# Context laid out with its features first, score maxima taken from two banks, one context load asked for earlier

## The reference

```python
x = x + xattn(layernorm(x), ctx, ctx)   # 32 query heads over 8 key/value groups of width 16, 512 context rows per batch
x = x + attn(layernorm(x))              # the same heads over the 32 tokens of the batch, causal, with rotary embedding
x = x + ffn(layernorm(x))               # one 512x512 matrix of 3-bit weights with a norm per 32, and a bias
```

## Time and profile before

| what | us |
|---|---|
| median of 3 runs | 349.91 |
| lowest and highest run | 349.44 and 350.54 |
| span of the profiled execution | 348.0 |
| PE busy in that span | 332.6 |
| DVE, ACT, POOL busy | 223.0, 192.1, 112.3 |

### The profile page before, as it was taken

The page is one execution under the profiler, slowest core; times in us unless marked ns, Lnnn a source line. Parts: engine busy times, 40 slices in busy tenths (PEclk is TensorE's granted clock), DMA queues, the critical chain, the costliest instruction groups (busy, mean ns, idle before and its releaser), DMA issues.

```text
span 348.0 us, 8374 instructions
## 1 busy us (share of the span) xinstructions
PE 332.6 (96%) x2930; PEld 240.3 (69%) x2930; DVE 223.0 (64%) x392; ACT 192.1 (55%) x369; POOL 112.3 (32%) x202
## 2 busy tenths in 40 slices
PE   7999785999999999999999999999899999999996
PEld 3764553777777777777777777777656866876664
DVE  1877673767667667586676766765766349876552
ACT  3553232676676666775766677765965612434220
POOL 1340831341331322413313123133551144663320
PEclk9999998999999999999999999999999999999999
DMA  7990298865777649869697599795940000000002
GB/s 268 406 126 0 63 208 191 173 116 153 108 186 153 121 154 125 176 155 113 172 179 99 156 112 215 156 182 160 130 55 2 2 6 6 6 9 6 2 32 90
DMA packets 40796, 41.52 MB, mean 119 GB/s; under 512 B 20112, under 2 KB 35472, under 8 KB 38672
## 3 DMA queue, kind: packets, MB, share of 16 engines
q1 hardware_dynamic: 40336, 41.00, 56.4%
q10 hardware_dynamic: 432, 0.13, 0.2%
HBM read 24.07 MB, written 1.05 MB: 72 GB/s over the span
## 4 chain that ended last, share of the span: by engine, by line
PE 85%; DVE 5%; DMA 2%; SPq 2%; ACT 2%; issue 1%; POOL 1%; ACTq 0%; DVEq 0%; POOLq 0%
PE b_d L1032 8%; PE b_c L1091 8%; PE b_s L1053 8%; PE b_v L1007 4%; PE b_c L1227 4%; PE b_k L1009 4%; PE b_k L1007 4%; PE b_k L1008 4%; PE b_v L1009 4%; PE b_v L1008 4%; PE b_x L979 4%; PE b_t L979 3%; DMA kstack<-kparts 2%; PE b_c L1212 2%; PE b_v L1058 2%; PE b_v L1117 1%
## 5 line engine op out<-in xcount | busy, mean ns | idle before, releaser
L789 DVE TENSOR_REDUCE negmax<-b_s 128x1 f32<-128x512 f32 x128 | 88.0, 688 | 70.6 <-PE b_s L1053 63.1
L594 ACT ACTIVATE region<-b_c 128x512 f32<-128x512 f32 x128 | 74.6, 597 | 53.6 <-PE b_c L1091 32.3
L1053 PE MATMUL b_s<-kstack,qstack 96*128 96x512 bf16 x128 | 49.5, 387 | 7.9 <-DMA kstack<-kparts 3.6
L1091 PEld LDWEIGHTS b_c<-qstack,kstack 108*128 108x128 bf16 x512 | 32.7, 98 | 26.6 <-issue 21.7
L1091 PE MATMUL b_c<-qstack,kstack 108*128 108x128 bf16 x512 | 50.5, 222 | 0.0
L476 POOL TENSOR_TENSOR mwide<-negmax,zeros 128x4 bf16<-128x4 f32 x32 | 6.4, 199 | 108.7 <-DVE negmax L789 108.7
L467 POOL TENSOR_TENSOR kparts<-kres,zeros 128x512 bf16<-128x512 f32 x16 | 18.9, 1180 | 40.3 <-DVE kres L774 40.3
L1007 PE MATMUL b_v<-cT_h,wkv_h 128*128 128x512 f32 x64 | 31.3, 489 | 0.0
L1032 PE MATMUL b_d<-region,vaug 128*17 128x128 f32 x1024 | 31.1, 273 | 0.0
L1007 PE MATMUL b_k<-cT_h,wkv_h 128*128 128x512 f32 x64 | 30.8, 481 | 0.0
L1032 PEld LDWEIGHTS b_d<-region,vaug 128*17 128x17 f32 x1024 | 26.6, 97 | 1.8 <-issue 0.2
(11 more groups left out here) (380 smaller groups left out, 663.8 us busy)
## 6 DMA issues: line engine op xcount, KB each, us to landing
cx<-in_ctx_dram SPq DMA_DIRECT2D x16, 1024.0 KB, 4.9
kstack<-kparts SPq DMA_DIRECT2D x96, 128.0 KB, 4.5
qstack<-region SPq DMA_DIRECT2D x76, 32.0 KB, 3.0
xs<-in_x_dram SPq DMA_DIRECT2D x1, 1024.0 KB, 8.1
region<-in_L_xattn_Wq_dram SPq DMA_DIRECT2D x1, 1024.0 KB, 10.2
cx<-in_L_xattn_Wo_dram SPq DMA_DIRECT2D x8, 128.0 KB, 4.3
cx<-in_L_attn_Wq_dram SPq DMA_DIRECT2D x1, 1024.0 KB, 5.4
region<-in_L_attn_Wo_dram SPq DMA_DIRECT2D x8, 128.0 KB, 7.4
```

The source lines that it names most:

```text
L594: nc.scalar.activation(pT[:, g], b_c[g % 2][:].rearrange("p (a n) -> p a n", a=KT), ACT.Exp, scale=SCALE).then_inc(exp_ready, 1)
L789: nc.vector.tensor_reduce(negmax[:, n % 2, g:g + 1], b_s[:], AX, ALU.max, negate=True).then_inc(max_ready, 1)
L1053: nc.tensor.matmul(b_s[:], qstack[0:STACK, g, n % 4], kstack[0:STACK, n % 4, g], start=True, stop=True).then_inc(s_ready, 1)
L1091: last = nc.tensor.matmul(b_c[g % 2][:, P * a:P * a + P], kstack[0:ROWS, m % 4, g, P * a:P * a + P], qstack[0:ROWS, g, m % 4], start=True, ...
```

## The change

The host hands over the context with features first (each batch transposed), Wq and Wk already in the order that the kernel used to make on the chip, and both output matrices in the order of the heads, so that their loads are one DMA each in place of eight. On the chip:

- `load_ctx` brings 4 features x 512 rows to each partition; ACT and DVE make `cT_h` and `cT_l` straight from that tile in SBUF. All 256 context transposes on PE go (16 in the opening for batch 0, 240 of line 979). Loads now wait for `ctx_low` (the chunks have been split) instead of `ctx_transposed`.
- Scores of odd groups go to bank `b_x` in slots before 14 (`score_bank`), so PE waits for the maximum two groups back, not one.
- Batch 0's context comes as four DMAs with a semaphore each. Batch 3's context is loaded in the opening, before the first query DMAs, not in slot 0.
- The reordering copies of Wq and the strided ones of Wk go. PE's warm-up is 9 matmuls, not 14, and the four after the context turn go.

```diff
+        first_ctx = [sem(f"first_ctx{c}") for c in range(C - 1)]
...
+        def score_bank(n, g, trip):
+
+            return b_x if g % 2 and (looped(trip) or n < B - 2) else b_s
...
-                sp.dma_start(cx[:, m % 2], ctx_d[4 * trip + m].rearrange("(p a) d -> p a d", a=KT)).then_inc(ctx_loaded[m % 2], 16)
+                sp.dma_start(cx[:, m % 2], ctx_d[4 * trip + m].rearrange("(p c) k -> p c k", c=C)).then_inc(ctx_loaded[m % 2], 16)
...
-                load_ctx(0, 0)
-                sp.dma_start(wkv_raw[:, 1], xwv_d.rearrange("(c p) m -> p c m", p=P)).then_inc(wv_loaded, 16)
+                first = ctx_d[0].rearrange("(p c) k -> p c k", c=C)
+                for c in range(C):
+                    sp.dma_start(cx[:, 0, c], first[:, c]).then_inc((*first_ctx, ctx_loaded[0])[c], 16)
+                sp.dma_start(wkv_raw[:, 1], xwv_d.rearrange("(p c) m -> p c m", c=C)).then_inc(wv_loaded, 16)
...
-                sp.wait_ge(ctx_transposed, C)
+                sp.wait_ge(ctx_low, C)
                 load_ctx(2, 0)
...
+                sp.wait_ge(ctx_low, 2 * C)
+                load_ctx(3, 0)
                 for part, done in ((0, q_high), (2, q_low)):
                     sp.wait_ge(done, R)
...
-                if live(n + 3, trip):
-                    sp.wait_ge(ctx_transposed, transposed)
+                if live(n + 3, trip) and (looped(trip) or n > 0):
+                    sp.wait_ge(ctx_low, halved)
                     load_ctx(n + 3, trip)
...
-                    sp.wait_ge(ctx_transposed, C * (B - 1))
-                    for g in range(G):
-                        sp.dma_start(wo[HD * g:HD * g + HD],
-                                     xwo_d[R * HD * g:R * HD * (g + 1)].rearrange("(r d) n -> d r n", r=R)).then_inc(weights_loaded, 16)
+                    sp.wait_ge(ctx_low, C * (B - 1))
+                    sp.dma_start(wo, xwo_d).then_inc(weights_loaded, 16)
...
-                pool.wait_ge(xwq_loaded, 16)
-                for c in (2, 3):
-                    nc.gpsimd.tensor_copy(wq_dg[:, c].rearrange("p r (d g) -> p r d g", g=G),
-                                          xwq[:, c].rearrange("p (g r d) -> p r d g", g=G, r=R)).then_inc(wq_ordered, 1)
...
-                        wait(act, ctx_transposed, C, m, c + 1, trip)
+                        if c == 0:
+                            wait_ring(act, ctx_loaded, m, trip)
                         wait(act, v_chunk, C, m - 1, c + 1, trip)
-                        nc.scalar.activation(cT_h[:, c], b_tx[c % 2][:], ACT.Copy).then_inc(ctx_high, 1)
+                        nc.scalar.activation(cT_h[:, c], cx[:, m % 2, c], ACT.Copy).then_inc(ctx_high, 1)
...
-                        nc.vector.tensor_reduce(negmax[:, n % 2, g:g + 1], b_s[:], AX, ALU.max, negate=True).then_inc(max_ready, 1)
+                        nc.vector.tensor_reduce(negmax[:, n % 2, g:g + 1], score_bank(n, g, trip)[:], AX, ALU.max, negate=True).then_inc(max_ready, 1)
...
-                        nc.vector.tensor_tensor(cT_l[:, c], b_tx[c % 2][:], cT_h[:, c].bitcast(F32), ALU.subtract).then_inc(ctx_low, 1)
+                        nc.vector.tensor_tensor(cT_l[:, c], cx[:, m % 2, c], cT_h[:, c].bitcast(F32), ALU.subtract).then_inc(ctx_low, 1)
...
-                        wait(pe, max_ready, G, n, g, trip)
-                        nc.tensor.matmul(b_s[:], qstack[0:STACK, g, n % 4], kstack[0:STACK, n % 4, g],
+                        wait(pe, max_ready, G, n, g - 1 if looped(trip) or n < B - 2 else g, trip)
+                        nc.tensor.matmul(score_bank(n, g, trip)[:], qstack[0:STACK, g, n % 4], kstack[0:STACK, n % 4, g],
                                          start=True, stop=True).then_inc(s_ready, 1)
...
-                    for second in range(2):
-                        ctx_ahead(n, g, second, trip)
-                        if n == B - 2:
+                    if n == B - 2:
+                        for second in range(2):
                             weight_part(g // 2, 2 * (g % 2) + second)
...
-                warm(14)
-                pe.wait_ge(ident_loaded, 16)
-                first_context(0)
-                first_context(1)
-                first_context(2)
-                first_context(3)
-                warm(4)
+                warm(9)
                 pe.wait_ge(wk_split, 1)
...
-                next_context(1, 0)
-                next_context(1, 1)
-                first_queries_of(0)
-                next_context(1, 2)
-                first_queries_of(1)
-                next_context(1, 3)
-                first_queries_of(2)
-                first_queries_of(3)
+                for r in range(R):
+                    first_queries_of(r)
...
-                next_context(2, 0)
```

More of the change, by code:

```diff
@@ L391, in slot @@
                 if looped(trip):
-                    passed, transposed, split = (
+                    passed, halved, split = (
                         sp.snap(step * trip + base) for step, base in
@@ L396, in slot @@
                 else:
-                    passed, transposed, split = G * (n - 1), C * m + C, m + 1
-                if live(n + 3, trip):
-                    sp.wait_ge(ctx_transposed, transposed)
+                    passed, halved, split = G * (n - 1), C * m + C, m + 1
+                if live(n + 3, trip) and (looped(trip) or n > 0):
+                    sp.wait_ge(ctx_low, halved)
                     load_ctx(n + 3, trip)
@@ L709, in opening @@
                 act.wait_ge(wk_loaded, 16)
[L710 to L711 removed]
+                nc.scalar.activation(wkv_h[:, 0], wkv_raw[:, 0], ACT.Copy).then_inc(wk_high, 1)
                 context(0, 0)
@@ L970, in _ @@
         def _(pe):
-            def ctx_part(m, c, a, trip):
-                if a == 0:
-                    if c == 0:
-                        wait_ring(pe, ctx_loaded, m, trip)
-                    wait(pe, ctx_low, C, m, c - 1, trip)
-                    if not looped(trip) and (m, c) == (1, 1):
-                        pe.wait_ge(xhT_ready, 1)
-                piece = nc.tensor.transpose(b_tx[c % 2][:, P * a:P * a + P], cx[:, m % 2, a, P * c:P * c + P], ident[:])
-                if a == KT - 1:
-                    piece.then_inc(ctx_transposed, 1)
             def weight_part(c, t):
@@ L1212, in warm @@
                     nc.tensor.matmul(b_c[1][:], zeros[:, 0:P], zeros[:], start=True, stop=True)
-            def first_context(c):
-                if c == 0:
-                    pe.wait_ge(ctx_loaded[0], 16)
-                for a in range(KT):
-                    last = nc.tensor.transpose(b_first[c][:, P * a:P * a + P], cx[:, 0, a, P * c:P * c + P], ident[:])
-                last.then_inc(ctx_transposed, 1)
             def first_queries_of(r):
                 pe.wait_ge(xhT_ready, TILES)
-                pe.wait_ge(wq_ordered, C)
+                pe.wait_ge(xwq_loaded, 16)
                 count(pe, q_res, r - 1)
                 for c in range(C):
-                    last = nc.tensor.matmul(b_c[r % 2][:], wq_dg[:, c, r], xhT[:, c], start=(c == 0), stop=(c == C - 1))
+                    last = nc.tensor.matmul(b_c[r % 2][:], xwq[:, c, r], xhT[:, c], start=(c == 0), stop=(c == C - 1))
                 last.then_inc(q_summed, 1)
-            def next_context(m, c):
-                for a in range(KT):
-                    ctx_part(m, c, a, 0)
             def opening():
                 pe.wait_ge(zeros_ready, 1)
-                warm(14)
-                pe.wait_ge(ident_loaded, 16)
-                first_context(0)
-                first_context(1)
-                first_context(2)
-                first_context(3)
-                warm(4)
+                warm(9)
                 pe.wait_ge(wk_split, 1)
@@ L1290 @@
     arrays = {name: _np.ascontiguousarray(inputs[name]) for name in _INS}
+    turned = lambda name, shape, axes: _np.ascontiguousarray(arrays[name].reshape(shape).transpose(axes))
+    arrays["ctx_4096"] = turned("ctx_4096", (B, KEYS, D), (0, 2, 1))
+    arrays["L0_xattn_Wq"] = turned("L0_xattn_Wq", (D, G, R, HD), (0, 2, 3, 1)).reshape(D, R, P)
+    arrays["L0_xattn_Wk"] = turned("L0_xattn_Wk", (D, G, HD), (0, 2, 1)).reshape(D, KV)
+    for name in ("L0_xattn_Wo", "L0_attn_Wo"):
+        arrays[name] = turned(name, (G, R, HD, D), (0, 2, 1, 3)).reshape(KV, R, D)
     arrays["L0_ffn_weight_q3"] = arrays["L0_ffn_weight_q3"].view(_np.int32)
```

52 lines of the change are left out of this document (16 added, 36 removed).

## The result

The changed kernel takes 337.89 us (median; 335.09 to 338.57), the kernel before on the same chip 349.68 (348.64 to 350.54): a ratio of 0.9654, interval 0.9612 to 0.9697. It is faster, as forecast, but by 12 us and not by 28, and 337.9 lies above the range of 317 to 333. The profiled span went from 348.0 to 336.7 us (the execution of 338.57).

What follows compares the result with a forecast made beforehand. PE was taken to bound the middle slots. Opening 3.0, slot 0 3.3, slot 1 3.4, middle slots 17.5 and slot 13 0.6 sum to 27.8 us off the 348.0 span: 320.2, so 322 us as median, range 317 to 333.

Steps and rivals of the forecast that it cites:

- rival 1: Middle slots: DVE's split stands behind POOL's key parts at the shared port, PE waits 1.2 us a slot; 336 us, chance 0.12.
- rival 2: Middle slots: ACT and DVE chains take over, PE waits for values and exponentials, slot stays 13.2 us; 330 us, chance 0.10.
- Rival 3: Every slot's first score waits for late-landing keys, so the kernel gets slower; 360 us with landings of 10, chance 0.03.
- I charge 0.2: Middle slots: lost cover at the turn of the values costs 0.2 us, making the slot 12.5 us instead of 12.33.
- I place the last split's end near 10.8: 1 us earlier: Opening: batch 0's context splits end 1 us earlier; part of the 3.0 us forecast gain to the first score.
- ACT then waits for Wv: Opening: between context splits ACT waits for Wv, whose DMA now stands behind the four context quarters.
- The stated lower bound of 0: Opening: the 3.0 us gain falls to 0 if PE's clock is still at the lower level in the first projections.
- The stop: Slot 0: DVE's split, reading SBUF twice, stands until POOL's multiply is done, 39.4 to 43.05 us.
- Nothing but DVE bounds it: Slot 0: DVE's 8 maxima, 4 splits and a copy alone set its length; forecast gain 3.3 us.
- a landing of 4.5 makes 10.2, under 12.5: Middle slots: keys made 5.7 us after the slot's first score land within the slot, so nothing is charged.
- took back 1.4 us for the clock: Slot 1: the 1.4 us cost of PE's half-clock start disappears; part of the 3.4 us forecast gain.
- batch 3's early load: Slot 0: loading batch 3's context before the queries costs a 0.6 us issue and lets slot 1's keys land at 48.8.

Runs made afterwards that it cites:

- the opening's two edits: Changed kernel with Wv's DMA right behind Wk's and seven more warm-up matmuls before the third projection chunk of batch 0; together, first score at 41.95 us (44.02 without).
- POOL's weights: Changed kernel with POOL's multiply and subtraction over the feed-forward weights moved out of the opening, in eight parts each in slots 0 and 1; 333.0 us.
- POOL's parts: Changed kernel with POOL's two multiplies and subtractions of 2048 elements cut into eight of 256 each, at the same places; 334.5 us.
- one bank: Changed kernel with one score bank instead of two by turns, each score waiting for the maximum just before it; 343.3 us.

## Why the prediction was wrong

The mechanism was right: PE bounded the slots, the turns were worth 0.22 us a pair, and a middle slot could go to 12.46. Neither of the rivals that stand for the middle (rival 1 at 336, rival 2 at 330) was the cause as they put it, and that 337.9 lies nearest to rival 1 is chance: in the middle slots no split that delayed PE is seen, and ACT is at 9.31 of 12.84 us. Rival 1 did name a late value copy, but by the port, and rival 2 DVE's chain, but by ACT's lines. Rival 3, dismissed at 0.03, was half right: keys land late, but in slots 2 and 14 only.

- **Middle slots, 3.8 of the missing 16.5 us.** The step "I charge 0.2" looked at PE's wait for ACT's copy before the turn alone. Behind the turn DVE's copy frees `b_v`, and ahead of it in DVE's order stand a maximum and the normalisation; the prediction doesn't name that wait. It costs 0.38 us a slot, shown by the run with the copy first. The 0.2 itself was about right: 12.46 in that run, against 12.33 without any wait.
- **Opening, 5.4 us.** "I place the last split's end near 10.8: 1 us earlier", with the statistics of x right behind, never asked when x lands. It had landed at 10.3 in the kernel before, and the change sends it 1.3 us later. "ACT then waits for Wv" was said and priced at next to nothing; it was 3.26 us. And the half clock, put down as a bound only, was real: the removed turns and warm-up matmuls were what PE did before these projections. The stated lower bound of 0 excluded a loss without a reason.
- **Slot 0, 2.0 us.** The stop came as forecast; but from its end (49.02) to slot 1's first score it is 8.2 us, where the prediction's eleven DVE instructions make 6.7: PE, at half clock until 55, bounds the rest. "Nothing but DVE bounds it" left that out, though the earlier trace rows has the same thing in slot 1.
- **Slot 1, 5.0 us.** The one sum for the keys, "a landing of 4.5 makes 10.2, under 12.5", stands with the middle slots and takes the median of all key DMAs; for slot 1, in which 1.2 MB is sent ahead of them, the wait for keys was put at nothing. With 8.31 the sum is 14.0, and slot 1 lasted 14.11. I also took back 1.4 us for the clock; PE stood still again, one slot later. And batch 3's early load, costed as a help, loses 2.3 us to slot 2's product against the changed kernel's profile (0.8 to 3.2 against the six runs that leave this stretch alone).
- **Slot 13, 0.4 us.** Keys again, 0.24 us of wait at slot 14's first score, which the sum had at nothing (and 4 x 0.22 less 0.2 is 0.7, not 0.6); what makes that wait small here and up to 2.6 us in other runs stays open. From slot 14 nothing was lost, as forecast.

With the opening's two edits, the copy, the keys, POOL's weights and the last layer's Wk and Wv put in the new order, the change gives 327.0 us. What keeps it from 322 is the opening (42.2 us to the first score; 38.6 was forecast), and slot 2, whose context is late once the keys go first (14.24 us).

## What to carry to other kernels

When work leaves the engine that bounds a loop, list for every buffer who frees it and what stands ahead of the freeing instruction in its own engine's order; the next wait is there, and a swap of two instructions can be worth as much as part of the change. Take a transfer's landing from the stretch in question, with the bytes that go out beside it, never as a median over the kernel; a shorter slot has the same bytes in less time. In an opening, ask of every input when it lands before asking when an engine could start on it.

## What was not expected of the hardware

- In the opening the granted clock is printed as 1.00 (12 to 14 us, and 14 to 16) while the same matmuls stand 0.42 us apart. The trace holds no record of the clock there before 17.76 us, and where it has none the column prints 1.00. From the first record on the two agree: in slot 2 (73.37 to 74.23) the column shows 0.50, with 0.43 between starts. So ahead of the first record the distance between starts, not the column, tells the clock.
- The clock's course in the opening differs between runs that are alike up to there. After the change and in three others the matmuls stand 0.42 us apart until 17.3 to 17.9. In four (POOL's parts, one bank, batch 3's context in slot 0, POOL's weights moved) they stand 0.23 apart from 7.6 us at the latest; the next ones, behind the third split, start 3.9 to 4.7 us later, and the clock is at 0.50 from 11.5 to 13.3 on until 15.6 to 18.3. In all eight the matmuls behind that split run at half clock, for 2.9 us or more.
- The key DMAs, from tile to tile in packets of 0.9 KB in the mean (528 packets, 0.48 MB), move little for the share of the queues that they take: from 50 to 54 us after the change, with nothing else going out on SP, the DMA share is 1.16 at 119 GB/s, while from 70 to 72, with a context load, 352 GB/s take a share of 0.95. A slot's keys (768 KB, by 119 GB/s some 6.6 us: an estimate) so hold the queues longer than its context of 1 MB (by 352 GB/s some 3.0).
